# An LSTM with a mixture of experts behind it, on one core: the four gate products in one scale, the tanh of the o gate kept in PSUM, and the sums of f and g taken without factors

## The reference

```python
x = x + _L0_cond_ref(x, cond_1024, L0_cond_Wx, L0_cond_Wh, L0_cond_b)
x = x + _L1_cond_ref(x, cond_1024, L1_cond_W_router, L1_cond_router_bias, L1_cond_s_w1, ...)
...
# L0: an LSTM of 256 units, h0 = cond, c0 = 0
xW = jnp.einsum('ntd,dk->tnk', x, Wx) + b
def step(carry, xw_t):
    prev_h, prev_c = carry
    a = xw_t + prev_h @ Wh
    i = jax.nn.sigmoid(a[:, :Hdim])
    f = jax.nn.sigmoid(a[:, Hdim:2 * Hdim])
    o = jax.nn.sigmoid(a[:, 2 * Hdim:3 * Hdim])
    g = jnp.tanh(a[:, 3 * Hdim:])
    next_c = f * prev_c + i * g
    next_h = o * jnp.tanh(next_c)
    return ((next_h, next_c), next_h)
_, hs = jax.lax.scan(step, (h0, c0), xW)
```

## Time and profile before

| | us |
|---|---|
| median of 3 runs | 1882.99 (1882.64 to 1883.02) |
| the profiled execution | 1883.11 |
| its span, first to last instruction | 1881.0 |
| mean granted TensorE clock in it | 0.998 of full speed |
| busy: PE, DVE, ACT, POOL | 1807.7, 1543.4, 855.9, 121.8 |
| L676, once in each step | x1024, from 20.3 to 1849.6 |

### The profile page before, as it was taken

One profiled execution on the slowest core, in us unless ns is written; L12 is line 12 of the kernel. 1 busy time (PEld: TensorE's weight loads), 2 busy tenths in 40 slices (PEclk: granted clock), 3 DMA queues, 4 the chain that ended last, 5 costly groups with the idle time before them and its releaser, 6 DMA issues.

```text
span 1881.0 us, 111282 instructions
## 1 busy us (share of the span) xinstructions
PE 1807.7 (96%) x45655; PEld 1605.0 (85%) x45655; DVE 1543.4 (82%) x13319; ACT 855.9 (46%) x5545; POOL 121.8 (6%) x404
## 2 busy tenths in 40 slices
PE   9999999999999999999999999999999999999999
PEld 8888888888888888888888888888888888888888
DVE  7888888888888888888888888888888888888885
ACT  4564444444444444444444444444444444444442
POOL 0000000000000000000000000000000000000000
PEclk9999999999999999999999999999999999999999
DMA  3300000000000000000000000000000000000000
GB/s 134 97 26 4 4 7 4 7 4 4 6 4 7 4 4 7 4 6 4 7 4 4 7 4 7 4 4 7 4 7 4 4 7 4 7 4 7 4 4 7
DMA packets 8448, 20.85 MB, mean 11 GB/s; under 512 B 1280, under 2 KB 5760, under 8 KB 7552
## 3 DMA queue, kind: packets, MB, share of 16 engines
q1 hardware_dynamic: 7504, 13.60, 2.2%
q10 hardware_dynamic: 432, 0.13, 0.0%
HBM read 11.63 MB, written 2.10 MB: 7 GB/s over the span
## 4 chain that ended last, share of the span: by engine, by line
DVE 44%; PE 41%; ACT 10%; issue 5%; DVEq 0%; PEldq 0%
PE gates L860 16%; DVE gates L676 8%; DVE gates L660 8%; ACT gates L371 7%; PE gates L878 7%; DVE to L692 7%; PE gates L867 6%; DVE addend L672 5%; DVE hh L697 4%; DVE gates L693 3%; DVE gates L688 3%; PE acc_lg L904 2%; PE up_rt L898 2%; PE gates L886 2%; DVE hid_rt L645 2%
## 5 line engine op out<-in xcount | busy, mean ns | idle before, releaser
L878 PE MATMUL gates<-hh,wh_lo 128*128 128x24 f16 x8184 | 783.1, 183 | 0.0
L878 PE MATMUL gates<-hh,wh_hi 128*128 128x24 f16 x8184 | 783.1, 183 | 0.0
L878 PEld LDWEIGHTS gates<-hh,wh_hi 128*128 128x128 f16 x8184 | 549.4, 96 | 0.0
L878 PEld LDWEIGHTS gates<-hh,wh_lo 128*128 128x128 f16 x8184 | 548.3, 95 | 0.0
L371 ACT ACTIVATE gates<-gates 128x4 f32<-128x4 f32 x1024 | 161.8, 158 | 825.2 <-DVE gates L660 824.8
L860 PEld LDWEIGHTS gates<-hh,wh_lo 128*128 128x128 f16 x8184 | 271.6, 96 | 266.6 <-DVE hh L697 264.7
L886 PE MATMUL gates<-hh,wh_small 128*128 128x2 f16 x8184 | 489.0, 164 | 0.0
L860 PE MATMUL gates<-hh,wh_lo 128*128 128x24 f16 x8184 | 380.3, 184 | 68.7 <-DVE hh L697 14.0
L660 DVE TENSOR_TENSOR_SCAN gates<-part_fac,gates 128x8 f32<-128x8 f32 x2048 | 295.6, 179 | 157.8 <-PE gates L867 132.4
L867 PE MATMUL gates<-hh,wh_hi 128*128 128x4 f16 x8184 | 370.3, 171 | 0.0
L886 PEld LDWEIGHTS gates<-hh,wh_small 128*128 128x128 f16 x8184 | 349.4, 96 | 0.0
(11 more groups left out here) (231 smaller groups left out, 2592.4 us busy)
## 6 DMA issues: line engine op xcount, KB each, us to landing
sw_sb<-sw SPq DMA_DIRECT2D x6, 512.0 KB, 4.0
rw_sb<-rw SPq DMA_DIRECT2D x2, 1024.0 KB, 5.7
rw_sb<-rw SPq DMA_DIRECT2D x4, 512.0 KB, 3.7
x_sb<-xT SPq DMA_DIRECT2D x1, 1920.0 KB, 9.5
outT<-osb SPq DMA_DIRECT2D x15, 128.0 KB, 2.2
wh_sb<-wh SPq DMA_DIRECT2D x2, 512.0 KB, 4.3
wx_sb<-wx SPq DMA_DIRECT2D x1, 1024.0 KB, 6.8
x_sb<-xT SPq DMA_DIRECT2D x1, 128.0 KB, 4.6
```

The lines of the kernel that those rows point to most:

```text
L878: mm(copies(q, m, LOW_COPIES)[:, :, :, 1], part, hh[:, c, half:half + 1, :].broadcast_to([P, LOW_COPIES, B]), start=False, stop=False, ski ...
```

## The change

All four gates now have their products in one scale, h times 4096: the high half of h is made from `to1`, which holds that factor, so the low half is full h minus high half. The matmuls that used `wh_small` use `wh_hi`; their number, shape and order stay. The sum of a pair needs no factor and becomes a reduction over pairs into 4 columns. `to` moves from SBUF to PSUM, into the bank of the o gate. The setup loses three passes on ScalarE, two scale constants and two memsets.

```diff
-        g_sum, f_sum = (beside(q, HC * PARTS) for q in (G, F))
+        g_sum, f_sum = (beside(q, HC) for q in (G, F))
+        to = beside(O, HC)
...
-                activation(to[:], o_sum, ACT.Tanh, scale=by_unit).then_inc(s_tanh, 1)
+                activation(to, o_sum, ACT.Tanh, scale=by_unit).then_inc(s_tanh, 1)
...
-            for dst, by in ((wh_g, 2.0), (wh_g_lo, 2.0 * LO), (s_wh, 1.0), (s_wh_lo, LO), (unit, 2.0)):
+            for dst, by in ((wh_g, 2.0), (s_wh, 1.0), (unit, 2.0 * LO)):
...
-            def lo_of(lo, hi, at):
+            def lo_of(q, n, by, at):
+
+                w = slice(q * D, (q + n) * D)
                 dve.wait_ge(s_hi, at)
-                v.scalar_tensor_tensor(wh_lo[:, :, lo:hi], wh_hi[:, :, lo:hi], -LO, wh_times_lo[:, :, lo:hi],
-                                       ALU.mult, ALU.add).then_inc(s_lo, 1)
+                v.scalar_tensor_tensor(wh_lo[:, :, w], wh_sb[:, :, w], by, wh_hi[:, :, w], ALU.mult, ALU.subtract).then_inc(s_lo, 1)
...
-                return v.tensor_tensor_scan(dst, part_fac[:].rearrange("p c j -> p (c j)"), parts[q], 0.0, ALU.mult, ALU.add)
+                return v.tensor_reduce(dst, parts[q].rearrange("p (c j) -> p c j", j=PARTS), AX.X, ALU.add)
...
                 dve.wait_ge(s_tanh, 3 * n + TO_OF)
-                v.tensor_scalar(to1[:], to[:], 1.0, LO, ALU.add, ALU.mult).then_inc(s_own, 1)
+                v.tensor_scalar(to1[:], to, 1.0, LO, ALU.add, ALU.mult).then_inc(s_own, 1)
                 v.tensor_copy(parts[O], seeds[:, piece % 2, at, O * HC:I * HC, :].rearrange("p c j -> p (c j)"))
 
+                dve.wait_ge(s_own, 2 * n + 1)
                 dve.wait_ge(s_tanh, 3 * n + TC_OF)
                 if not final:
-                    v.scalar_tensor_tensor(h_hi, by_batch(to[:]), 1.0, by_batch(tc), ALU.add, ALU.mult).then_inc(s_hhi, 1)
+                    v.tensor_tensor(h_hi, by_batch(to1[:]), by_batch(tc), ALU.mult).then_inc(s_hhi, 1)
 
                 h_now = h32[:, piece % 2, at, :]
-                dve.wait_ge(s_own, 2 * n + 1)
                 v.tensor_tensor(h_now, to1[:], tc, ALU.mult).then_inc(s_own, 1)
...
                 dve.wait_ge(s_own, 2 * n + 2)
-                v.scalar_tensor_tensor(h_lo, h_hi, -LO, by_batch(h_now), ALU.mult, ALU.add).then_inc(s_hlo, 1)
+                v.tensor_tensor(h_lo, by_batch(h_now), h_hi, ALU.subtract).then_inc(s_hlo, 1)
...
-                        last = mm(copies(q, m, n)[:, :, :, 1], wh_small[:, c, w], hh[:, c, 0:1, :].broadcast_to([P, n, B]),
+                        last = mm(copies(q, m, n)[:, :, :, 1], wh_hi[:, c, w], hh[:, c, 0:1, :].broadcast_to([P, n, B]),
```

More of the change, by code:

```diff
@@ L140, in cond_resid_kernel @@
         wh_lo = sb("wh_lo", [P, KC, H4], F16)
-        wh_small = sb("wh_small", [P, KC, 2 * D], F16)
         wx_part = [sb("wx_hi", [P, KC, H4], F16), sb("wx_lo", [P, KC, H4], F16)]
@@ L165, in cond_resid_kernel @@
         tops, s_wh, s_wx, s_xin = scale[:, 0, :], scale[:, 3, 0:1], scale[:, 3, 1:2], scale[:, 3, 2:3]
-        sc = sb("sc", [P, 7])
-        unit, two_unit, to_tanh, half_lo, s_wh_lo, wh_g, wh_g_lo = (sc[:, j:j + 1] for j in range(7))
+        sc = sb("sc", [P, 5])
+        unit, two_unit, to_tanh, half_lo, wh_g = (sc[:, j:j + 1] for j in range(5))
         xw_scale = sb("xw_scale", [P, 2])
@@ L172, in cond_resid_kernel @@
         first_banks = (*(gates[:, q * BANK:(q + 1) * BANK] for q in (G, F)), up_sh, up_rt, xw_next, gates[:, O * BANK:(O + 1) * BANK])
-        wh_times_lo = xw[:, TS * GATES:TS * GATES + KC * H4].rearrange("p (k n) -> p k n", k=KC)
         hw0 = sb("hw0", [P, GATES])
@@ L178, in cond_resid_kernel @@
         seeds = sb("seeds", [P, 2, HS, GATES, PARTS])
-        part_fac = sb("part_fac", [P, HC, PARTS])
         addend = sb("addend", [P, HC, 3])
         c_now = sb("c_now", [P, HC])
-        to = sb("to", [P, HC])
         to1 = sb("to1", [P, HC])
@@ L324, in finish @@
                 take_back(pool, s_added, 2 * PIECES)
-            pool.wait_ge(s_scale, 5)
+            pool.wait_ge(s_scale, 3)
             stage(0, slice(GATES, (HS + 1) * GATES))
@@ L343, in _ @@
             nc.scalar.preload_act_table(ACT.Gelu)
[L345 to L360, removed]
+            act.wait_ge(s_scale, 2)
+            for q, n, by in ((G, 1, wh_g), (F, 3, s_wh)):
+                activation(wh_hi[:, :, q * D:(q + n) * D], wh_sb[:, :, q * D:(q + n) * D], ACT.Identity, scale=by).then_inc(s_hi, 1)
+            act.wait_ge(s_scale, 4)
             by_unit = nc.scalar.alloc_register("by_unit")
             nc.scalar.reg_load(by_unit, to_tanh[0:1, :].bitcast(U32))
-            def last_of(sums):
-                return sums.rearrange("p (c j) -> p c j", j=PARTS)[:, :, PARTS - 1]
             def lstm(s):
                 act.wait_ge(s_sum, 3 * s + F_OF)
-                activation(tf, last_of(f_sum), ACT.Tanh, scale=by_unit).then_inc(s_tanh, 1)
+                activation(tf, f_sum, ACT.Tanh, scale=by_unit).then_inc(s_tanh, 1)
                 act.wait_ge(s_sum, 3 * s + G_OF)
-                activation(addend[:, :, 0:2], last_of(g_sum).rearrange("p (c o) -> p c o", o=1).broadcast_to([P, HC, 2]),
+                activation(addend[:, :, 0:2], g_sum.rearrange("p (c o) -> p c o", o=1).broadcast_to([P, HC, 2]),
                            ACT.Tanh, scale=by_unit).then_inc(s_scan, 1)
@@ L389, in first_tile @@
                     n, m = XW_FIRST[s]
-                    if s == 0:
-                        act.wait_ge(s_lo, 3)
                     act.wait_ge(s_xwp, s + 1)
@@ L487, in _ @@
             link(v.memset(seeds[:], 0.0))
-            link(v.memset(part_fac[:, :, 0], 0.0))
-            link(v.memset(part_fac[:, :, 1], 1.0 / LO))
             link(v.memset(ones[:], 1.0))
@@ L511, in _ @@
             dve.wait_ge(s_link, done[0])
-            for dst, by in ((wh_g, 2.0), (wh_g_lo, 2.0 * LO), (s_wh, 1.0), (s_wh_lo, LO), (unit, 2.0)):
+            for dst, by in ((wh_g, 2.0), (s_wh, 1.0), (unit, 2.0 * LO)):
                 v.tensor_scalar(dst, scale[:, 2, 0:1], 2.0 ** 13 * by, None, ALU.mult).then_inc(s_scale, 1)
-            link(v.tensor_scalar(two_unit, scale[:, 2, 0:1], 2.0 ** 15, None, ALU.mult))
+            link(v.tensor_scalar(two_unit, scale[:, 2, 0:1], 2.0 ** 15 * LO, None, ALU.mult))
             v.reciprocal(to_tanh, two_unit).then_inc(s_scale, 1)
@@ L537, in _ @@
                 if m == 1:
-                    lo_of(0, D, 2)
+                    lo_of(G, 1, wh_g, 1)
                 if m == 2:
-                    dve.wait_ge(s_hi, 3)
-                    v.scalar_tensor_tensor(wh_lo[:, :, 2 * D:H4], wh_sb[:, :, 2 * D:H4], s_wh, wh_hi[:, :, 2 * D:H4],
-                                           ALU.mult, ALU.subtract).then_inc(s_lo, 1)
+                    lo_of(O, 2, s_wh, 2)
                 if m == 5:
-                    lo_of(D, 2 * D, 4)
+                    lo_of(F, 1, s_wh, 2)
             dve.wait_ge(s_xwc0, MC)
@@ L756, in first_tile @@
                     i = LO_OF[s]
-                    dve.wait_ge(s_hi, 5 + i // 2 + 1)
+                    dve.wait_ge(s_hi, 2 + i // 2 + 1)
                     v.scalar_tensor_tensor(wx_slice(wx_part[1], i, 2 * NW), wx_slice(wx_sb, i, 2 * NW), s_wx,
@@ L884, in and_low @@
                     for c in range(KC):
-                        w = slice(((q - O) * KC + m) * P, ((q - O) * KC + m + 1) * P)
-                        last = mm(copies(q, m, n)[:, :, :, 1], wh_small[:, c, w], hh[:, c, 0:1, :].broadcast_to([P, n, B]),
+                        w = slice((q * KC + m) * P, (q * KC + m + 1) * P)
+                        last = mm(copies(q, m, n)[:, :, :, 1], wh_hi[:, c, w], hh[:, c, 0:1, :].broadcast_to([P, n, B]),
                                   start=False, stop=True, skip_group_check=True)
@@ L1087, in _ @@
                         pe.wait_ge(s_lo, 3)
-                        pe.wait_ge(s_hi, 5)
                     lstm(s, 0)
```

## The result

The changed kernel takes 1961.82 us (median of 4 runs, 1960.98 to 1964.62), the kernel before in the same comparison 1882.83 (1882.64 to 1883.02): a ratio of 1.0422, interval 1.0409 to 1.0435. That is 79 us more. The forecast was 1954, with 1941 to 1975 as its range.

The account below looks back on a forecast made before the run. A loop of waits through VectorE, TensorE and ScalarE was taken as the bound, 1.788 us a step. +0.078 - 0.008 = +0.070 us, times 1023 = +71.6 us on 1883, gave 1954, range 1941 to 1975.

Parts of the forecast that it names:

- The main term: The high half's second wait, for tanh c, unfulfilled in an instruction of its own: +0.078 us a step, bounds 0 to 0.09.
- own range: The forecast's spread with the wait at 0.07 to 0.09 and the operation at 0.151 to 0.159: 1946 to 1975 us.
- The upper end: If the extra instruction carried the wait for `to1` instead, the high half would start at 1002.92, 0.02 later.
- The o side: Tanh o into PSUM, `to1` from it at 0.155: high half 0.012 later by itself, hidden behind the second wait.
- Rival A: Second wait absorbed, so tanh o and `to1` decide: +0.004 a step, 1887 us (1883 with `to1` at 0.151); chance 7%.
- rival D: PSUM reads as dear as the skill's table has them: `to1` later, high half 0.02 later, some 1972 us; chance 4%.
- The high half's form: High half as a tensor_tensor, 0.151 as L701 instead of 0.159: -0.008 us a step, bounds -0.008 and 0.
- The sums: Sums of f and g as reductions, 0.152 instead of 0.179: f's addend 0.027 earlier, worth 0 in the loop.
- The tie that I called TensorE's: Addend of f and tanh i end together ahead of the c scan, tanh i held by TensorE's products of i.
- rival B: Wait absorbed; f sum, not tanh i, held c side: 0.027 + 0.008 off each step, 1847 us; chance 3%.
- rival C: TensorE's clock at the lower level in four steps at each of 15 tile changes: 58 us more, 2012; chance 6%.

Follow-up runs that it names:

- e3: Kernel before with one wait moved: the high half also waits for `to1`, ahead of tanh c; 1961.15 us, ratio 1.0421.
- e1: Changed kernel with `to1` raising the tanh counter, so the high half has one wait; 1903.65 us, ratio 1.0115.
- e2: Changed kernel with the two waits ahead of the high half in the other order; 1985.62 us, ratio 1.0548.
- e6: Changed kernel with tanh o written to SBUF again instead of PSUM; 1963.16 us, ratio 1.0426.
- e5: Changed kernel with scale 1, the high half made from `to` and `tc` again, `to` in SBUF, no second wait; 1879.24 us, ratio 0.9979.
- e9: e5 with the sums of f and g made by scans again, results at every second place; 1884.77 us, ratio 1.0008.
- e4: Kernel before with one more, long fulfilled wait per step ahead of the high half; 1888.29 us, ratio 1.0029.
- e8: Kernel before with one small ordinary VectorE instruction more per step, behind the copy of i's seed; 1883.97 us, ratio 1.0000.

## Why the prediction was right

**The main term** was right in mechanism: the second wait became an instruction of its own and was unfulfilled. It was 9 ns too large. I took 0.078 for a wait that is an instruction of its own; it is 102 - 33 = 69 ns, just under the "0.07 to 0.09" of the own range. The two rows behind it were single ones, rounded to 0.01. e3 shows that it makes the slowdown by itself, e1 that it goes with the instruction, e2 that it follows the wait that is written second.

**The upper end** ("0.02 later" if the extra instruction carried the other wait) was e2: 24 to 25 ns a step, 24 us.

**The o side.** Without the extra instruction `to1` was to make the high half 0.012 late. (The sum as it stands gives 0.018: 1002.46 + 0.158 + 0.03 + 0.155 + 0.035 = 1002.838 against 1002.82; with the medians of the records it gives 0.011.) e1 measures 20 ns (it starts at x + 1327 instead of 1307). The 8 to 9 ns from 11 to 20 are nearly all `to1` itself: I took 0.155, and it is 163 in e1 (161 in the changed kernel):

```profile
L668 DVE TENSOR_SCALAR to<-gates x1024: 150/163/163, 20.8 to 1870.5; 128x4 f32<-128x4 f32 x171
```

In the changed kernel this is hidden, as predicted: `to1` has 80 ns where 34 would do, and e6 takes 23 of them for 2 ns a step. Rival A's 1887 would have been e1's 1904.

**The PSUM table** (rival D). `to1` from PSUM takes 161 to 163 ns, from SBUF 170: by the Trainium skill, "VectorE: DVE Perf Modes", TRN2 errata, the PSUM form should be dearer, and here it is not. The measurement decides.

**The high half's form.** -8 ns was expected, and +2 measured (480 to 482). The row that I took 0.151 from, L701, wasn't a measure for it: the tensor_tensor takes 157 against 159, and TensorE starts its low-weight products 216 ns behind the high half's start before and after. The 2 ns aren't placed: e5, which has the old form, has 482 too, and e1, with the new one, 480.

**The sums.** This step failed. A reduce was to take 0.152 and to be worth nothing, since the c scan "waits for tanh i too" and that waits for TensorE. The reduce takes 175 against the scan's 179; its mean in the page (with the first and last of each pair):

```profile
L636 DVE TENSOR_REDUCE gates<-gates 128x4 f32<-128x8 f32 x2048 | 291.0, 174 | 158.1 <-PE gates L843 132.9
```

The row that I borrowed, with one output column, wasn't of its shape. And it isn't worth nothing: tanh i's end hangs on tanh g, hence on g's sum, 5 to 6 ns a step (e9). The tie that I called TensorE's was VectorE's and ScalarE's as well, and the addend of f didn't come ready 0.03 ahead of tanh i but together with it. Had the reduce been as quick as I took it, rival B's mechanism might have won something; no run shows that.

**The late steps** were in no term: +11.4 us; where they lie is told below. From forecast to result, at 1.02 us for each ns of a step: the wait 9 less, the sums 5 less, the high half to the next x 10 more than I took, and the late steps: -9 - 5 + 10 + 11 = +7, so 1954.6 becomes 1962, where 1961.8 was measured. That the forecast came within 8 us is partly luck, since these offset each other: the typical step was forecast 4 ns too long, and the late steps not at all.

**The clock** (rival C) held but for one stretch (columns as in the earlier trace rows):

```profile
1092.00:1095.90 3.90, 3.01 (x89) 2.63 (x86) 3.24 (x27) 1.30 (x12) 0.40 (x1) 1.00 0.01 2
```

```profile
1095.90:1099.30 3.40, 3.40 (x60) 2.67 (x56) 2.47 (x22) 1.30 (x10) 0.89 (x3) 0.50 0.17 43
```

For 3.4 us the granted clock was 1.2 of 2.4 GHz; steps 575 and 576 were 0.79 us over the median together, which is within the 12.3. They are step 63 of a tile and step 0 of the next, where rival C put it, behind a step 574 that was late by 0.23, and TensorE was busy for 3.01 of the 3.90 us ahead of the fall; but it is one of the 15 changes of tiles. Two of the three executions without a trace have a mean granted clock of 0.997 and took 1961.70 and 1961.93 us, the third 0.998 and 1960.98: they may have had such a stretch too.

**Where the late steps lie.** The traces say more of this than the experiments. I number VectorE's entries of a trace from 0, those that only wait or only raise a counter included. Over the eleven traces, 213 steps behind step 64 are late. In 211 of them the lateness begins at an entry whose number is 63 modulo 128; the other two are the two of the clock. In the kernel before such an entry stands 43 times on one of the five instructions from the high half to the seed of i, and is never late there. In the changed kernel it does so 41 times, in e4 29 times, and it is late every time. What is fixed is how soon it can start behind the entry of the extra wait (medians in ns):

| instruction behind the extra wait | usual, changed kernel | usual, e4 | at a 128th place, changed kernel | at a 128th place, e4 |
|---|---|---|---|---|
| high half | 66 | 144 | 418 | 418 |
| h | 142 | 220 | 455 | 454 |
| next c | 210 | 289 | 492 | 494 |
| low half | 327 | 405 | 528 | 530 |
| seed of i | 407 | 484 | 564 | 566 |

That is 0.42 us and some 0.037 for each instruction between, whether the wait was fulfilled or not. An unfulfilled wait is passed 78 ns nearer to the high half, which is why the same steps are 73 to 83 ns later with it. L677 in the lines above is such an entry, and so is L702 of e4. The packets of q14 fit: 8 more for 1024 entries more are one for 128 entries.

**What stays open.** Why that entry is held. The rows call it issue. That VectorE gets its list in pieces of 128 entries, and has the next piece later where an entry that only waits has just passed, would fit; no run moves the border of a piece, so the place and the delay are shown and the mechanism isn't.

The 3 us by which some executions of several kernels differ, this one's profiled run included, lie ahead of the first step. In the three traces of the longer kind (the changed kernel, e8, e9) the first 22 products of `cond_sb` with `wh_sb` in the setup take 4.69 us together, in the eight others 2.5 to 2.8. What decides between the two isn't shown.

## What to carry to other kernels

On a loop that has no slack, count the waits of the instruction that closes it: one direct wait costs 33 to 34 ns from the event here, and one in an instruction of its own 69 ns more if its event comes last, once in every step. Let both events raise one counter (e1), or order the waits so that the one written second is the one long fulfilled; that one still brings late steps (e4: 5.4 us); and before making an operand "cheaper", see which counter it brings along. Where an operation seems released by one engine, look whether it also stands close behind its forerunner on its own engine: its end may hang on that one. And where single steps are late without a wait, number the engine's entries before looking for a cause in the data.

## What the runs showed of the hardware

- An unfulfilled wait in an instruction of its own: 36 to 38 ns from the event to it and 66 ns on to the instruction behind it, 102 to 104 in all (the changed kernel, e2, e3, e6), against 33 to 34 for a direct wait (the kernel before, e1). Fulfilled: 0 on a typical step (e4).
- With such an instruction ahead of a busy stretch of VectorE, 35 to 57 steps of 1023 are late, most by 0.1 to 0.35 us, at places that come again in kernels of the same layout (all 55 of e6 are among the 57 of the changed kernel). Behind step 64 the lateness begins at a 128th entry of VectorE's list (211 of 213 late steps in eleven traces). Close behind such an instruction that entry starts 0.42 us after it, and 0.037 later for each one between (the changed kernel, e2, e3, e4, e6).
- ScalarE's tanh of i ends 65 to 66 ns behind the tanh before it, whether its own record says 163 or 168 (the kernel before, the changed one, e5, e9).
- On four columns a tensor_scalar takes 161 to 163 ns from PSUM (the changed kernel, e1) and 170 from SBUF (the kernel before).
